# Row maxima of an attention kernel turned into rows by a DMA that transposes, with TensorE's sixteen-step order rewritten

## The reference

```python
x = x + attention(layernorm(x))
# in attention, for each of 4 sequences and 16 heads:
logits = einsum('bhnd,bhmd->bhnm', q, k) * 4.0
attn = softmax(logits, axis=-1)
h = einsum('bhnm,bhmd->bhnd', attn, v)
# then x = x + mix(layernorm(x))
```

## Time and profile before

| what | us |
| --- | --- |
| median of 3 runs | 2761.07 (2760.24 to 2761.52) |
| profiled execution, whole | 2761.08 |
| its span of instructions | 2759.3 |
| TensorE busy | 2725.5 (99%) |
| VectorE busy | 2497.6 (91%) |
| ScalarE busy | 2484.6 (90%) |
| GpSimd busy | 373.0 (14%) |

### The profile page before, as it was taken

One profiled execution on the slowest core, in us unless ns is written; L12 is line 12 of the kernel. 1 busy time (PEld: TensorE's weight loads), 2 busy tenths in 40 slices (PEclk: granted clock), 3 DMA queues, 4 the chain that ended last, 5 costly groups with the idle time before them and its releaser, 6 DMA issues.

```text
span 2759.3 us, 60096 instructions
## 1 busy us (share of the span) xinstructions
PE 2725.5 (99%) x23674; PEld 910.9 (33%) x23674; DVE 2497.6 (91%) x4853; ACT 2484.6 (90%) x2863; POOL 373.0 (14%) x751
## 2 busy tenths in 40 slices
PE   9999999999999999999999999999999999999999
PEld 6552222222222222222222222222222222224776
DVE  6659999999999999999999999999999999985774
ACT  7779999999999999999999999999999999997555
POOL 7760000000000000000000000000000000103451
PEclk9999999999999999999999999999999999999999
DMA  6641010100000000000010101010101100212531
GB/s 197 216 152 58 11 33 12 30 15 22 19 22 22 22 22 22 23 22 23 14 29 8 33 11 33 12 33 11 33 12 34 32 19 22 59 40 77 166 131 46
DMA packets 135290, 124.36 MB, mean 45 GB/s; under 512 B 49888, under 2 KB 117344, under 8 KB 135008
## 3 DMA queue, kind: packets, MB, share of 16 engines
q1 hardware_dynamic: 135008, 120.52, 14.1%
HBM read 72.75 MB, written 47.19 MB: 43 GB/s over the span
## 4 chain that ended last, share of the span: by engine, by line
PE 85%; SPq 5%; DVE 5%; ACT 3%; DMA 1%; issue 1%; ACTq 0%
PE psum L1378 34%; PE psum L1278 18%; PE psum L1338 16%; PE psum L1408 4%; DVE a_mx L1056 4%; PE psum L1876 3%; ACT a_copied L982 2%; PE psum L1293 2%; PE psum L1423 2%; PE psum L447 2%; SPq L153 2%; PE psum L1864 2%; DMA a_qs<-q_parts 1%; SPq L158 1%; SPq L126 1%
## 5 line engine op out<-in xcount | busy, mean ns | idle before, releaser
L1056 DVE TENSOR_REDUCE a_mx<-psum 128x1 f32<-128x512 f32 x3096 | 1930.3, 683 | 105.8 <-PE psum L1338 94.8
L1278 PE MATMUL psum<-a_qs,a_ks 50*128 50x512 f16 x4096 | 788.6, 383 | 4.7 <-ACT p_x L973 0.5
L973 ACT ACTIVATE m_gate<-psum 128x1024 f32<-128x1024 f32 x684 | 679.6, 1036 | 41.2 <-PE psum L1278 37.4
L973 ACT ACTIVATE p_x<-psum 128x1024 f32<-128x1024 f32 x682 | 678.0, 1036 | 39.8 <-PE psum L1278 36.4
L973 ACT ACTIVATE m_y<-psum 128x1024 f32<-128x1024 f32 x682 | 677.9, 1036 | 38.2 <-PE psum L1278 34.1
L1338 PE MATMUL psum<-a_ks,a_qs 48*128 48x512 f16 x3596 | 691.1, 383 | 17.7 <-DVE a_mx L1056 12.3
L1378 PE MATMUL psum<-m_gate,a_vst 128*32 128x512 f32 (+1 forms) x4576 | 413.5, 433 | 0.0
L1378 PE MATMUL psum<-p_x,a_vst 128*32 128x256 f32 (+1 forms) x4560 | 412.2, 433 | 0.0
L1378 PE MATMUL psum<-m_y,a_vst 128*32 128x512 f32 (+1 forms) x4560 | 412.2, 433 | 0.0
L1278 PEld LDWEIGHTS psum<-a_qs,a_ks 50*128 50x128 f16 x4096 | 196.3, 93 | 569.1 <-ACT p_x L973 137.3
L1051 DVE CUSTOM_DVE_ANT_0 a_copied<-psum,a_copied 128x512 f32<-128x512 f32 x500 | 324.2, 686 | 18.0 <-PE psum L1338 16.9
(11 more groups left out here) (149 smaller groups left out, 1639.1 us busy)
## 6 DMA issues: line engine op xcount, KB each, us to landing
m_x<-x SPq DMA_DIRECT2D x24, 512.0 KB, 5.5
a_qs<-q_parts SPq DMA_DIRECT2D x384, 32.0 KB, 2.1
sums<-a_o SPq DMA_DIRECT2D x256, 34.0 KB
q_parts<-m_split SPq DMA_DIRECT2D x16, 512.0 KB, 3.4
v_rows<-m_v SPq DMA_DIRECT2D x16, 512.0 KB, 2.8
k_parts<-m_split SPq DMA_DIRECT2D x16, 512.0 KB, 3.9
a_ks<-k_parts SPq DMA_DIRECT2D x64, 128.0 KB
a_vin<-v_rows SPq DMA_DIRECT2D x64, 128.0 KB, 5.6
```

Of the source, the lines that this page charges most:

```text
L973: ac.activation(p_sb[n % WEIGHTS][:, 2 * pair:2 * pair + 2, :], psum[:, at:at + 2, :], ACT.Exp, scale=SCALE).then_inc(s_exp, 1)
L1056: dve.tensor_reduce(peak, psum[:, bank(at), :], AX.X, ALU.max).then_inc(s_mx, 1)
L1278: mm = te.matmul(psum[:, pair_of_banks(u) + par, :], ks[row:row + MR, (it // QB) % 2, pair, c * P:(c + 1) * P], qs[row:row + MR, it % QRIN ...
```

## The change

The transpose on TensorE and its copy on ScalarE are gone from all blocks but the first. Instead SyncE waits for GpSimd's chain, issues one transfer of a 128 by 128 float16 square (`m_square`, whose first 32 columns are `m_parts`) with transposition into `m_rows`, waits for it to land, and issues the four row transfers as before. GpSimd's next split waits for that landing. GpSimd clears the unused 96 columns once at the start.

`even` and `odd` issue the same fills, packs and products in another order, and the larger packs and the copies stand elsewhere in their periods.

```diff
-    LARGER = ((5, 11), (4, 13))
-    COPY_AT = ((1, 15), (6, 12))
-    EXPS_BEFORE = ((1, 14), (6, 11))
+    LARGER = ((1, 11), (1, 10))
+    COPY_AT = ((1, 11), (1, 12))
+    EXPS_BEFORE = ((1, 10), (1, 11))
...
-    m_parts = sb("a_mparts", [P, PARTS, G * TT], F16)
-    m_rows = sb("a_mrows", [PARTS * G * TT, P], F16)
+    m_square = sb("a_mparts", [P, P], F16)
+    m_parts = m_square[:, 0:PARTS * G * TT].rearrange("p (a n) -> p a n", a=PARTS)
+    m_rows = sb("a_mrows", [P, P], F16)
...
             else:
-                sp.wait_ge(s_exp, turn_unit(it) + 1)
+                sp.wait_ge(s_ch, CHAIN * (it + 1))
+                sp.wait_ge(s_mr, M_INC * it)
+                sp.dma_start(m_rows[:, :], m_square[:, :], transpose=True).then_inc(s_turned, DMA)
+                sp.wait_ge(s_turned, DMA * it)
...
             elif pit:
-                pool.wait_ge(s_st, turn_unit(pit - 1) + 1)
+                pool.wait_ge(s_turned, DMA * (pit - 1))
...
+        pool.memset(m_square[:, PARTS * G * TT:P], 0.0).then_inc(s_one, 1)
...
-        def keep_rows(pit):
-            u = turn_unit(pit)
-            ac.wait_ge(s_st, u + 1)
-            ac.wait_ge(s_mr, M_INC * pit)
-            ac.copy(m_rows[:, :], psum[0:PARTS * G * TT, pair_of_banks(u), 0:P // 2].bitcast(F16)
-                    ).then_inc(s_exp, 1)
...
-        def turn(pit):
-
-            te.wait_ge(s_ch, CHAIN * (pit + 1))
-            u = turn_unit(pit)
-            after(te, s_exp, u - 1)
-            te.transpose(psum[0:PARTS * G * TT, pair_of_banks(u), 0:P // 2].bitcast(F16),
-                         m_parts[:, :, :].rearrange("p a n -> p (a n)"), ident[:, :]).then_inc(s_st, 1)
...
-            turn((p + 1) // 2)
```

More of the change, by code:

```diff
@@ L509, in stage_attend @@
     FILLS_AHEAD = 4
-    TURN_AT = 7
     APART = 5
@@ L635, in larger_pack @@
         return first_pack(LEAD + p // 2) + LARGER[(LEAD + p // 2) % 2][p % 2]
[L637 to L644, removed]
     def fill_of(period, e):
@@ L653, in unit @@
         copies = min(2 * period + sum(e >= n for n in EXPS_BEFORE[period % 2]), COPIES)
-        return 2 * n + pair + copies + turns_before(fill_of(period, e))
+        return 2 * n + pair + copies
     def copy_unit(p):
[L657 to L664, removed]
+        return FILLS * (p // 2) + COPY_AT[p // 2 % 2][p % 2]
     def pair_of_banks(u):
@@ L942, in keep_first_rows @@
             ac.wait_ge(s_turn0, 1)
-            ac.copy(m_rows[:, :], psum[0:PARTS * G * TT, VALUE, 0:P // 2].bitcast(F16)).then_inc(s_row0, 1)
-        def keep_rows(pit):
-            u = turn_unit(pit)
-            ac.wait_ge(s_st, u + 1)
-            ac.wait_ge(s_mr, M_INC * pit)
-            ac.copy(m_rows[:, :], psum[0:PARTS * G * TT, pair_of_banks(u), 0:P // 2].bitcast(F16)
-                    ).then_inc(s_exp, 1)
+            ac.copy(m_rows[0:PARTS * G * TT, :], psum[0:PARTS * G * TT, VALUE, 0:P // 2].bitcast(F16)).then_inc(s_row0, 1)
         def keep_projected(blk):
@@ L1452, in last_fills @@
             for f in range(first, fill_of(until // SPAN, until % SPAN * GP + last) + 1):
-                if turn_at(f) is not None:
-                    turn(turn_at(f))
                 fill(f)
@@ L1493, in even @@
             times_v(c + 2)
+            fill(f + 9)
             peaks(n + 5)
-            fill(f + 9)
+            fill(f + 10)
             times_v(c + 3, 0)
-            fill(f + 10)
             peaks(n + 6)
@@ L1503, in even @@
             times_v(c + 4, 0)
+            fill(f + 13)
             peaks(n + 8)
-            fill(f + 13)
             times_v(c + 4, 1)
@@ L1508, in even @@
             peaks(n + 9)
+            fill(f + 15)
             times_v(c + 5, 0)
-            fill(f + 15)
             peaks(n + 10)
@@ L1513, in even @@
             times_v(c + 5, 1)
+            fill(f + 17)
             peaks(n + 11)
-            fill(f + 17)
             times_v(c + 6, 0)
@@ L1518, in even @@
             peaks(n + 12)
+            fill(f + 19)
             times_v(c + 6, 1)
-            fill(f + 19)
             peaks(n + 13)
@@ L1523, in even @@
             times_v(c + 7, 0)
+            fill(f + 21)
             peaks(n + 14)
-            fill(f + 21)
             times_v(c + 7, 1)
@@ L1532, in odd @@
             peaks(n + 1)
+            fill(f + 5)
             times_v(c)
-            fill(f + 5)
             peaks(n + 2)
@@ L1537, in odd @@
             times_v(c + 1, 0)
+            fill(f + 7)
             peaks(n + 3)
-            turn((p + 1) // 2)
             times_v(c + 1, 1)
-            fill(f + 7)
+            fill(f + 8)
             peaks(n + 4)
-            fill(f + 8)
+            fill(f + 9)
             times_v(c + 2, 0)
             peaks(n + 5)
-            fill(f + 9)
+            fill(f + 10)
             times_v(c + 2, 1)
-            fill(f + 10)
+            fill(f + 11)
             peaks(n + 6)
             times_v(c + 3, 0)
-            fill(f + 11)
+            fill(f + 12)
             peaks(n + 7)
-            fill(f + 12)
+            fill(f + 13)
             times_v(c + 3, 1)
             peaks(n + 8)
-            fill(f + 13)
+            fill(f + 14)
             times_v(c + 4, 0)
-            fill(f + 14)
+            fill(f + 15)
             peaks(n + 9)
             times_v(c + 4, 1)
-            fill(f + 15)
+            fill(f + 16)
             peaks(n + 10)
-            fill(f + 16)
             times_v(c + 5)
@@ L1619, in tensor @@
         even(PERIODS - LEAD - 1)
-        for n in range(PACKS - -1, PACKS):
-            peaks(n)
         for n in range(SPAN * (PERIODS - LEAD), STEPS):
```

6 lines of the change are left out of this document (1 added, 5 removed).

## The result

The changed kernel takes 2764.84 us (median of 21 runs, 2762.30 to 2766.12), the kernel before 2761.06 (21 runs). The ratio is 1.0013, with a 95% interval of 1.0008 to 1.0019: 3.8 us slower, which is clear of noise and still within the 0.2% that the text ahead called the same. I had forecast 2755.8, a gain. The profiled execution has a span of 2762.9 us, 3.6 more than before.

The account below looks back on a forecast made before the run. Three nearly full engines bound the kernel, with 1.9 to 2.0 us of TensorE holds above a 34.2 us floor per block. 62 x 0.08 = 5.0 plus 0.3 in the tail: 2761.08 - 5.3 = 2755.8, range 2741 to 2770.

Parts of the forecast that it names:

- What bounds the kernel: Attention blocks of 36.16 us: PE, DVE and ACT nearly full, TensorE's floor 34.2, holds of 1.9 to 2.0.
- The floor of 34.2: TensorE's time in us for a block's 64 pairs and 27 products without holds, the same in both orders.
- the two rules: VectorE: tiles every 0.60, packs 0.75 after the previous first tile; ScalarE: instructions every 0.91, fills 1.07 after last-but-one's start.
- the walk: Row-by-row working out of holds through one even and one odd by the rules: block 36.08, steps good to about 0.02.
- The transpose, removed: Removing odd's transpose from TensorE gives back 0.14 to 0.34 us a block, 9 to 21 us in all.
- the hold of 0.13: In odd, the score behind the transpose waits for ScalarE's copy: 1030.82 where 1030.69 was possible.
- the one of 0.20 at the differences: In odd, the differences stand 0.43 behind the pack instead of 0.23; up to 0.12 hangs on the transpose.
- The transposing transfer, added: On SyncE between GpSimd's chain and the first score: takes 2.1 us, hidden by 8.3 us left, 8.0 by walk.
- My third rival, the transfer in the open: Transfer not hidden: beyond 8.0 us each microsecond costs one a block, up to about 5200 us; chance 0.03.
- The order, rewritten: Even loses 0.14 (17.83 for 17.69), odd takes 18.25 for 18.48; block 36.08, gain 0.08 to 0.09.
- The second rival: Slower: TensorE waits for ScalarE behind even's earlier copy, 0.14 a block, 8.7 us, 2770; chance 0.17.
- The sum: 62 blocks at 0.08 give 5.0, plus 0.3 for the tail's transpose: 2755.8 us, +-6; forecast's chance 0.52.

Follow-up runs that it names:

- e2_oldorder: Changed kernel with the order, larger packs and copies of the kernel before, only the transpose replaced by the transfer: 2760.12 us, ratio to before 0.9995.
- e3_neworder_turn: Kernel before with the new order, larger packs and copies, the transpose kept on TensorE behind odd's third pack: 2788.49 us, ratio to before 1.0099.
- e10_q_behind: Changed kernel with SyncE's load of queries issued behind the transposing transfer and rows in every block: 2761.69 us, ratio to before 1.0005.
- e4_late_hoist: e1_late with VectorE's wait for GpSimd's chain moved one pack earlier, ahead of odd's last tile: 2759.57 us, ratio to before 0.9994.
- e9_copy_later: e1_late with even's copy at fill 14 in place of 11 and its second larger pack at 11 in place of 10: 2763.82 us.
- e11_pack_first: e1_late with one swap in even, the fifth pack ahead of fill f+9 behind the whole product: 2756.53 us, ratio to before 0.9983.
- e1_late: Changed kernel with block 60's early loads moved on SyncE's queue behind the transposing transfer and rows: 2760.41 us, ratio to before 0.9998.
- e8_five: e1_late with the transposing transfer made five times in each block, one behind the other: 3092.09 us in one run.

## Why the prediction was wrong

**What bounds the kernel.** Right. The floor of 34.2, the two rules and the distance of 36.16 carried the walk: from the first pack of `even` (1009.50) the beginning of `odd` was forecast 17.83 later and stands at 1027.34, 17.84 later.

**The transpose, removed.** The mechanism was right, the size was under the lower bound: 0.10 a block in the old order, where I gave 0.14 to 0.34. I had taken the holds as TensorE's alone. In `odd` of `e2_oldorder` the hold of 0.13 is gone and the one of 0.20 at the differences is 0.09, but the packs at 1029.10 and 1030.29 now wait 0.08 and 0.09 for VectorE, where in the kernel before the same two wait nothing and 0.06. `e3_neworder_turn` shows that the price belongs to the place: 0.44 in the new order.

**The transposing transfer, added.** This step failed, and with it the sign. Its duration was taken well: 2.3 us to land in the median, 2.1 assumed, and hidden in steady blocks, where even two are. But "8.3 us are left" (8.0 by the walk), "which the cover hides", was read from one block and taken for all of them. The kernel before has the warning in the same place of SyncE's timeline:

```profile
2401.43 8.61 SPq L153 DMA_DIRECT2D a_qs<-q_parts  x6
2410.08 2.72 SPq L730 DMA_DIRECT2D a_qs<-a_mrows  x4
```

There the rows went out 6 us behind the chain's end already, and the first score of the next block stood at 2417.18. Between 2410.08 and 2417.18 are 7.1 us, of which the rows need 2.7 for issue and 1.1 to land (2418.75 to 2419.85 in the changed kernel): 3.3 us of room, and the transfer took 5.7. With the usual 2.3 to land, 1.0 would still have been left; and `e10_q_behind` shows that the landing beside the loads can cost a wait even when the issue is in time. My third rival, the transfer in the open, had the mechanism, but priced it for all blocks or none and gave it 0.03. One block, with the slower clock behind it, was enough: -5 became +4.

**The order, rewritten.** This step failed too: the walk's 36.08 is 36.14 in the trace, and the loop's gain of 5.0 us became 0.43. The loss in `even` of 0.14 came as forecast (17.84 against 17.69 before), with the waits of 0.09 and 0.20 for ScalarE where the walk had them (0.09 and 0.21). `odd` takes 18.30, where I had 18.25. Apart from the hold at 1045.64, which both kernels have, its largest is at its beginning:

```profile
1027.34 0.39 PE L1255 MATMUL psum<-a_qs,a_ks 50*128 50x512 f16 x2
1027.69 0.39 PE L1315 MATMUL psum<-a_ks,a_qs 48*128 48x512 f16 x2
1027.92 0.38 PE L1255 MATMUL psum<-a_qs,a_ks 50*128 50x512 f16 x2
...
1045.64 0.39 PE L1315 MATMUL psum<-a_ks,a_qs 48*128 48x512 f16 x2 [0.17 <-DVE a_mx L1033]
```

The pack stands 0.35 behind the score, where 0.23 is possible: a hold of 0.12, for which the prediction has 0.1. 0.06 x 62 = 3.7 us of the 5.0 are the walk's error, and 0.05 of the 0.06 lie in `odd`; the prediction does not give the walk's rows there, so at which of them the error arose stays open. The rest of the 5.0 went to the few longer blocks. What is shown of the place at the beginning: the pack is late because VectorE begins a block's first tile 0.06 later than others, and `e4_late_hoist` takes that away and gains only 0.01, because ScalarE holds the next score there. The rule for ScalarE was a little off in a long run of exponentials: their starts lie 0.90 apart, but each is recorded a little longer than the one before (1.03, 1.04 and 1.05 from 1020.72 on in `e9_copy_later`), so that the release comes later than 1.07 behind the start (1.10 in `e4_late_hoist`, 1026.46 to 1027.56).

The second rival had TensorE wait for ScalarE in the middle of `even` behind the earlier copy. The waits are there, but they stay when the copy is moved (`e9_copy_later`), and `e11_pack_first` recovers 0.06 of the 0.14 of `even` by putting a pack ahead of a score. For the other 0.08 no run shows the cause.

**The sum.** In the profiled executions 5.3 us less was forecast and 3.6 more came, 8.9 apart: 4.6 are the loop's missing gain and 4.1 the late block. Ahead of and in the first distance 0.7 was lost, and the tail gave 0.8 in place of 0.3. Without the late block the two kernels cannot be told apart, as `e1_late` shows; only with it is the changed one slower. +-0.1 us a block was wide enough for the walk, which missed by 0.06, but the +-6 in all left out a one-off. The range of 2741 to 2770 held the time only because it took in the rivals.

## What to carry to other kernels

In a loop of 62 passes a gain of 0.07 us in each is worth as much as one stall of 4.1 at its end: when a step is moved to another queue, read its room in the block where that queue is fullest, not in a typical one, and add the landing time beside the traffic of that block. When three engines are over 95% busy, a hold is worth only what remains until the next engine's hold; try the removal alone first, since here it beat the version with the order rewritten for it. Behind the longest instruction put first the work that feeds the engine that was idle meanwhile: here that was worth 0.07 a block.

## What the hardware showed that I had not expected

A wait of 2.65 us of TensorE was followed, after 1.4 us of work at full clock, by 3.5 us at a granted clock of 0.53, and it cost 4.1 us in all. In `e8_five` a wait of 4.0 us in a block was followed by 4.7 us at 0.64. A wait of 0.84 us in `e10_q_behind` was followed by full clock and cost 0.9. A transposing transfer of 128 by 128 float16 on an otherwise quiet queue was issued in 1.1 us and landed in 2.3; near loads of 256 and 512 KB on the same queue it took 5.7, 8.0 and 9.6. VectorE began a tile 0.48 behind its pack when the instruction waited for two semaphores, and 0.42 when it waited for one: `e4_late_hoist` moved the second wait away, and the tile began 0.42 behind.
